# Zero products in front of three of TensorE's waits in the far units of grouped attention

## The reference

```
x = x + global_latent_attn(rmsnorm(x, norm1_w), g_wq, g_kv_down, g_k_up, g_v_up, g_wo)
x = x + local_gqa_attn(rmsnorm(x, norm2_w), l_wq, l_wk, l_wv, l_wo)
...
scores = jnp.einsum('bhqd,bhkd->bhqk', q, k) / np.sqrt(HD).astype(np.float32)
scores = jnp.where(mask, scores, jnp.float32(-1e+30))
probs = jax.nn.softmax(scores, axis=-1)
return jnp.einsum('bhqk,bhkd->bhqd', probs, v)
```

## Time and profile before

| | us |
|---|---|
| median of three runs | 1625.4 |
| lowest, highest | 1624.96, 1625.66 |
| span of the profiled execution, first to last instruction | 1651.8 |
| TensorE busy in the span | 1306.4 (79%) |
| VectorE, GpSimd, ScalarE busy | 1040.1, 851.7, 816.2 |

### The profile page before, as it was taken

The page is one execution under the profiler, slowest core; times in us unless marked ns, Lnnn a source line. Parts: engine busy times, 40 slices in busy tenths (PEclk is TensorE's granted clock), DMA queues, the critical chain, the costliest instruction groups (busy, mean ns, idle before and its releaser), DMA issues. The chain is left out here.

```text
span 1651.8 us, 33458 instructions
## 1 busy us (share of the span) xinstructions
PE 1306.4 (79%) x11130; PEld 844.3 (51%) x11130; DVE 1040.1 (63%) x3079; ACT 816.2 (49%) x1378; POOL 851.7 (52%) x1271
## 2 busy tenths in 40 slices
PE   4774889936988888877899378888899996875688
PEld 3663778911333333337899223333355555643556
DVE  3675434447778878844354767766666624766876
ACT  1452222311666666652232156666655555765665
POOL 3367564434335555565554667666544313666543
PEclk9996899955999999988999579998999997998799
DMA  6201222258222333042221300000000000000001
GB/s 181 49 30 49 68 70 73 58 114 165 72 71 78 83 85 84 17 125 69 75 74 55 106 1 1 2 1 1 2 2 2 2 2 1 1 1 1 1 1 52
DMA packets 86292, 79.40 MB, mean 48 GB/s; under 512 B 11775, under 2 KB 76159, under 8 KB 85824
## 3 DMA queue, kind: packets, MB, share of 16 engines
q1 hardware_dynamic: 72290, 55.07, 13.6%
q0 software_dynamic: 8640, 17.84, 3.3%
q10 hardware_dynamic: 5196, 4.35, 1.3%
HBM read 45.94 MB, written 31.28 MB: 47 GB/s over the span
## 5 line engine op out<-in xcount | busy, mean ns | idle before, releaser
L1422 ACT ACTIVATE grp_pt<-ps 128x1024 f32<-128x1024 f32 (+2 forms) x320 | 244.3, 799 | 204.5 <-PE ps L1501 126.4
L2414 DVE TENSOR_REDUCE soft_mx<-ps 128x2 f32<-128x1024 f32 (+3 forms) x256 | 201.3, 818 | 59.6 <-PE ps L2217 57.2
L2095 ACT ACTIVATE arena<-ps 128x768 f32<-128x768 f32 (+1 forms) x192 | 166.9, 881 | 99.9 <-PE ps L2250 81.4
L1022 POOL DMA_INDIRECT products<-moe_product,moe_rows_in x142 | 136.9, 964 | 145.3 <-DVE moe_product L1115 133.2
L1039 ACT ACTIVATE moe_hid<-ps 128x512 f32<-128x512 f32 x142 | 84.4, 597 | 229.6 <-issue 107.9
L1068 PE MATMUL ps<-moe_rT,moe_W_now 128*128 128x128 f32 x1136 | 160.3, 287 | 20.7 <-DVE moe_rT L1107 13.0
L1996 POOL TENSOR_SCALAR_AFFINE_SELECT arena<-arena 128x256 f32<-128x256 f32 (+1 forms) x192 | 92.7, 485 | 143.9 <-ACT arena L2095 143.1
L1521 PE MATMUL ps<-grp_pt,grp_vpad 128*32 128x160 f32 (+4 forms) x2048 | 149.2, 401 | 16.0 <-POOL grp_pt L1363 15.7
L1068 PEld LDWEIGHTS ps<-moe_rT,moe_W_now 128*128 128x128 f32 x1136 | 146.3, 201 | 25.4 <-DVE moe_rT L1107 16.0
L841 POOL DMA_INDIRECT sorted_rows<-route_row,route_target x128 | 127.7, 997 | 34.2 <-issue 30.7
L1363 POOL TENSOR_SCALAR_AFFINE_SELECT grp_pt<-grp_pt 128x256 f32<-128x256 f32 (+1 forms) x192 | 105.5, 558 | 76.3 <-ACT grp_pt L1422 75.1
(11 more groups left out here) (362 smaller groups left out, 2838.9 us busy)
## 6 DMA issues: line engine op xcount, KB each, us to landing
moe_rows_in<-sorted_rows SPq DMA_DIRECT2D x142, 65.0 KB
route_stacks<-soft_scratch_k SPq DMA_DIRECT2D x32, 192.0 KB
arena<-products SPq DMA_DIRECT2D x8, 512.0 KB, 7.5
soft_scratch_q<-soft_parts SPq DMA_DIRECT2D x16, 192.0 KB, 2.8
route_stacks<-soft_scratch_q SPq DMA_DIRECT2D x32, 96.0 KB
arena<-products SPq DMA_DIRECT2D x4, 768.0 KB, 13.5
soft_scratch_k<-soft_parts SPq DMA_DIRECT2D x15, 192.0 KB, 2.8
products<-moe_product,moe_rows_in POOLq DMA_INDIRECT x142
```

The lines of the kernel that those rows point to most:

```text
L1022: pool.indirect_dma_start(k.products, bass.IndirectOffsetOnAxis(rows_in[:, s % RING, DEST_COL:DEST_COL + 1].bitcast(U32), 0), product[:, s ...
L1422: act.activation(at.pair(pt[:, s % 2, :], pair, seg)[:, :, 0:w], ring[(chunks_before(m) + c) % 2][:, :, 0:w], ACT.Exp, scale=scale).then_i ...
L2095: act.activation(LATENT.pair(pt[:, s % 2, :], pair, seg)[:, :, 0:w], ring[second_turn(n, c) % RING3][:, :, 0:w], ACT.Exp, scale=scale).the ...
L2414: ins = dve.tensor_reduce(mx[:, tile, half, :, r], ring[first_turn(n, d) % RING3][:, :, at:at + keys], AX.X, ALU.max)
```

## The change

A helper `keep_awake` issues a number of matmuls of 512 bf16 columns, whose stationary operand is a table of zeros, `nothing`, and whose moving operand is the table of ones, `onesb`, repeated four times. With start=False they add zero to what stands in the PSUM bank. In units 1 to 7 they stand between `scores` and `values_at`: three at chunk 0, three at chunk 2, five at chunk 19, all into `sums[1]`. The table takes the place of `causal_k`, which nothing read. No wait and no semaphore is added, and the other engines' instructions are the same in number and order.

```
+def keep_awake(pe, k, o, times, start=True):
+
+    for _ in range(times):
+        pe.matmul(o, k.nothing, k.onesb.unsqueeze(1).to_broadcast([P, T, P]), start=start, stop=True, skip_group_check=True)
...
             FAR = {"q": 2, "k": 4, "x": 6, "qkv": 8, "sums": 13, "back": 16, "out": 19}
+            AWAKE = {0: 3, 2: 3, 19: 5}
...
                 for c in range(plan(m).chunks):
                     scores(m, c)
+                    if 0 < m < B and c in AWAKE:
+                        keep_awake(pe, k, sums[1], AWAKE[c], start=False)
                     values_at(m, c)
...
-    k.causal_k = sb("causal_k", [P, P], BF16)[:, :]
+    k.nothing = sb("nothing", [P, P], BF16)[:, :]
...
-                               (k.causal_k, "causal_k"), (k.before, "before")):
+                               (k.nothing, "nothing"), (k.before, "before")):
...
-        "causal_k": bf(np.where(query < key, NEG, 0.0)),
+        "nothing": bf(np.zeros((P, P))),
```

## The result

| | before | after |
|---|---|---|
| median of 9 runs | 1624.96 us (1616.12 to 1629.43) | 1613.27 us (1610.78 to 1617.54) |
| ratio | | 0.9937, 95% interval 0.9912 to 0.9962 |
| span of the profiled execution | 1651.8 | 1614.7 |
| the `turn_q` called in unit 1 to the `output` called in unit 8 (the stretch) | 220.04 | 204.79 |
| mean clock in the stretch | 0.91 | 1.00 |

The kernel is faster by 0.63% (0.38 to 0.88), which is 10 us (6 to 14); the medians lie 11.7 apart. The forecast was 1612.0 against a median of 1625.4, 13.4 less.

The account below looks back on a forecast made before the run. Each unit was taken as a loop through all engines, slowed where TensorE is late at low clock. Gains of 7.6, 2.2 and 3.9 us made 13.7, taking 1625.4 to 1611.7, say 1612 us; range 1608.5 to 1621.

Parts of the forecast that it names:

- The mechanism: Units 1 to 7: products shrink TensorE's pauses at chunks 19 and 2, so the clock stays at 2.4 GHz; chance 0.60.
- Cost 0 for the products: Chunks 0, 2 and 19: the products fit in TensorE's waits of 1.74 and 1.34 to 1.67 us, costing 0.
- the cheap end of 0.21: Each new product: lowest estimated time, 512 columns at 2.4 GHz, 0.21 us.
- the dear end of 0.27: Each new product: highest estimated time, scaled from a 480-column pair with its changeover, 0.27 us.
- `turn_q` to `output`, 7.6 us: Units 2 and 4 to 7: gain from `turn_q` at full clock, 1.51 and 1.54, then 1.54 + 1.52 + 1.50; 7.6 us.
- `output` to `turn_q`, 6.1 us: From `output` to the next `turn_q`: units 1, 2, 4 gain 2.2 us, units 5 to 7 gain 3.9.
- the high end: Units 5 and 6, after `output`: TensorE's own work saves 1.5 us up to the next unit's first `scores`.
- VectorE still had to norm and add there (units up to 4 only): After `output` in unit 3: part of the saving was lost to this work; units 5 and 6 lack it, so 1.3.
- The total: Whole kernel: 13.7 us gained, taken over whole from the profiled span to the median of 1625.4.
- The products do not hold the clock: Units 1 to 7: products of zeros leave the falls as before and lie in the waits; 1625.4 us, chance 0.12.
- One of the two falls stays: Either the fall behind chunk 2 stays (1619.3 us, 0.14) or that at chunk 19 (1617.8 us, 0.07); chance 0.21.
- Slower: the products run at the low clock: Chunks 0, 2 and 19: at 1.2 GHz products outlast the waits, about 10 us lost, 1635 us; chance 0.07.

Follow-up runs that it names:

- x2: The changed kernel with only the five products at chunk 19: stretch 211.76 us, 5 falls, ratio to before 0.9959.
- x3: The changed kernel with only the three products at chunk 0 and three at chunk 2: stretch 207.61 us, 2 falls, ratio to before 0.9934.
- x5: The changed kernel with the same eleven products 32 columns wide in place of 512: stretch 222.00 us, 12 falls, one run.
- x10: The changed kernel with the table of zeros but no products, run a second time and timed: stretch 219.31 us, 11 falls, ratio to before 0.9985.
- x4: The changed kernel with products doubled to six, six and ten at chunks 0, 2 and 19: stretch 210.18 us, no fall, ratio to before 0.9988.
- x6: The changed kernel with its eleven products moved to chunks 3, 5 and 7, into `sums[0]`: stretch 240.66 us, 11 falls, one run.
- x1_table_only: The changed kernel with the table of zeros but no products, first execution: stretch 215.76 us, 8 falls, one run.
- x7: The changed kernel with only three products at chunk 2 and three at chunk 19: stretch 206.57 us, 1 fall, ratio to before 0.9915.
- x8: The changed kernel plus eight products at each of chunks 8 and 16 of unit 0: stretch 205.31 us, no fall, ratio to before 0.9943.
- x9: The changed kernel itself, run again on the second chip: stretch 205.18 us, no fall, ratio to before 0.9919.

## Why the prediction was right

**The mechanism** held. Eleven falls became none. The products at a place keep the clock up at that place (x2, x3); that they also change what happens at the other (x3) was not foreseen. The narrow products rule out that anything else in the edit did it (x5), the table alone that the table did (x10).

**Cost 0 for the products.** Right: `output` to `turn_q` in unit 3, undisturbed in both traces, is 9.44 before and 9.45 after, and `turn_q` to `output` 18.72 in both. The room at chunk 19 was as small as worked out, 0.49 in unit 5, and doubling costs 0.77 us a unit (x4). At chunks 0 and 2 there was more of it in unit 4 than the 1.74 us that were read in unit 5 to 6, behind a slow `output`. Behind the fast one of unit 3 TensorE waited 1.65 for the mask (to 1069.51) and then the 0.84 at 1071.21 of the earlier trace rows, 2.49 together. The change makes that the rule in units 2 to 4, and it fits that the six added products of x4 cost nothing there. A product inside a row of ten took 2.17/10, 0.22 us, with no wait behind it (x4), near the cheap end of 0.21; outside the waits and with the changeovers it was 0.28 (x6), just over the dear end of 0.27.

**`turn_q` to `output`, 7.6 us.** Measured 1.51 + 1.54 + 1.55 + 1.54 + 1.52 in units 2 and 4 to 7, 7.7.

**`output` to `turn_q`, 6.1 us.** Measured 7.6: the mis-sized term. Units 1 and 2 gave 0.81 and 0.61 as forecast, unit 7 about 1.35 for 1.3 (1183.23 to 1203.83 before, 1142.30 to 1161.55 after). Unit 4 gave 1.68 for 0.78, and units 5 and 6 1.67 and 1.48 for 1.3 each. Of unit 5's 1.67, 1.51 lie before the first `scores` of the next unit (1087.38 to 1091.55 is 4.17), as the high end had it, and 0.16 behind it. The step that failed is "VectorE still had to norm and add there (units up to 4 only)". `add_back` ends one unit earlier, with unit 3; `apply` alone, in unit 4, does not hold GpSimd up. GpSimd and VectorE after the change, unit 3 first and then GpSimd in unit 4:

```profile
1035.21 2.10 POOL L1369 TENSOR_SCALAR_AFFINE_SELECT grp_pt<-grp_pt 128x256 f32<-128x256 f32 x2 [0.65 <-ACT grp_pt L1428]
1037.27 1.34 POOL L1351 CAST grp_quad<-grp_unit 128x1024 f16<-128x1024 f32 x1
...
1035.33 0.68 DVE L1606 TENSOR_TENSOR x<-arena,x 128x512 f32<-128x512 f32 x1
1036.05 0.78 DVE L1608 TENSOR_TENSOR x<-arena,x 128x512 f32<-128x512 f32 x1
...
1063.38 0.46 POOL L1369 TENSOR_SCALAR_AFFINE_SELECT grp_pt<-grp_pt 128x256 f32<-128x256 f32 x1 [0.65 <-ACT grp_pt L1428]
...
1064.67 1.35 POOL L1351 CAST grp_quad<-grp_unit 128x1024 f16<-128x1024 f32 x1
```

In unit 3 two masks take 2.10 us from 1035.21, while VectorE does its two additions to x at L1606 and L1608; in unit 4 a mask of the same form takes 0.46. The cast for `turn_q` (L1351) then starts 5.46 us after `output` in unit 3 (1031.81 to 1037.27) and 4.69 in unit 4 (1059.98 to 1064.67), which is 0.77 of the 0.9 us between 9.45 and 8.54. That the additions slow the masks is argued from their lying side by side; it was not tried apart, and in x10_table_again a mask of this form that began at 1010.12, beside the same additions, took 0.41.

**The total.** 15.25 in the two profiled traces, 13.4 as the mean of five traces, 13.7 forecast, and 10 (6 to 14) and 13 (8 to 19) timed. That 13.7 lies so near to 13.4 is partly luck: the forecast priced the eleven falls of one trace and was some 1.5 too low for it, and three traces without products had 11, 8 and 11 falls, so that the mean gain is 1.9 less than in that trace. That the timed value of the first is lower is within its interval. One thing that widens the interval can be seen in the traces: after the stage the clock falls as well, in the MLP and Toeplitz stages, and this part took from 293.35 us at a clock of 0.89 (before) to 299.56 at 0.86 (x1_table_only), with and without products alike (299.08 in x7, 293.41 in x8, 298.44 after). The first and the last of these in windows, the table alone and unit 0:

```profile
1348.09:1647.65 299.56, 223.59 (x1200) 159.98 (x1200) 203.14 (x774) 183.58 (x418) 151.97 (x227) 0.86 0.03 8
```

```profile
1342.69:1636.10 293.41, 215.74 (x1200) 154.52 (x1200) 202.96 (x774) 183.51 (x418) 151.82 (x227) 0.89 0.03 8
```

**The rivals.** "The products do not hold the clock" is refuted: products whose stationary operand is a table of zeros (the moving one is ones) held it in all seven units, in four traces of three kernels (after, x9, x8, x4). The sentence of the Trainium skill (TensorE: Matmul & The Clock Gate, Part 1) on zero operands is about another limiter, and a like blindness was not seen here. "One of the two falls stays" came about only where its products were left out, and once where those at chunk 0 were (x7); the rule of the Trainium skill (same page, Part 4) that the full clock does not engage for PE-mode transposes is not borne out by the trace of after: behind the products all seven `turn_q` ran 16 transposes in 1.07 us. "Slower: the products run at the low clock" did not come about, since no group of the change began at the low clock; x6 shows what it would have been, 1.37 us for three in place of 0.82.

## What to carry to other kernels

Where a matrix engine that sets the pace pauses for a microsecond or two at fixed places of a loop, compare iterations whose products after the pause are slow with those where they are fast: here the difference was about 1.4 us a fall (15.25 over 11), and it is what filling the pause can bring. Count the falls in more than one execution: the same kernel had 8 in one and 11 in others. Fill only what the wait leaves, with work that no other engine waits for: the same eleven products brought 13 us inside the waits and cost 22 beside them, and where the engine isn't late (unit 0) they bring nothing. Read such an effect from a stretch of the trace that begins and ends at fixed instructions; the whole time scattered here by 13 us without any change (1616.12 to 1629.43). Compare traces from one chip: the two chips here differ by 20 to 27 us ahead of the stretch.

## What was not expected of the hardware

- With `turn_q` at the full clock the pause of 1.34 or 1.67 us before `output`, unfilled, led to a fall in only 2 of 7 units (x3), against 6 of 7 in the kernel before.
- Without products the number of falls varied from execution to execution, 8 in x1_table_only and 11 in x10_table_again, and the steps at the low clock ended by degrees (1.89, 1.82, 1.61, 1.37, 1.07 us).
- Two of GpSimd's masks of 128x256 took 2.10 us beside VectorE's additions, and one took 0.40 to 0.53 elsewhere in the stretch of the same trace (after).
